# A graph-attention layer with its steps reordered on three engines, its self loop's sum on VectorE and two scalings on ScalarE

## What is computed

```python
x_l = x @ W_l + b_l
x_r = x @ W_r + b_r
e_emb = ea @ W_e                              # edges, and one self loop per node with the mean weight
m = leaky_relu(x_l[src] + x_r[tgt] + e_emb, 0.2)
logits = einsum(m, att)
alpha = softmax(logits) over the edges of a target
out = gelu(segment_sum(alpha * x_l[src]) + bias)
h = out + x
h = (h - mean(h)) * rsqrt(var(h) + 1e-5) * ln_w + ln_b     # the inner norm
x = layernorm(x + h)                                       # its scaling is left to the last layer
```

## Time and profile before

| | |
|---|---|
| median of 3 runs | 3335.7 us (3334.68 to 3337.22) |
| profiled execution: its time | 3335.34 us |
| profiled execution: its span | 3333.5 us |
| TensorE, VectorE, ScalarE, GpSimd busy | 78%, 80%, 60%, 57% of the span |
| mean granted TensorE clock | 0.903 |
| DMA | 611.76 MB, mean 184 GB/s |

### The profile page before, as it was taken

How to read it: one execution, slowest core, us unless ns; L and a number is a source line. 1 busy time by engine, 2 the same in 40 slices (tenths; PEclk the granted TensorE clock), 3 DMA queues, 4 the chain that set the end, 5 groups by cost and what they waited for, 6 DMA issues and landing times. The chain is left out here.

```text
span 3333.5 us, 45939 instructions
## 1 busy us (share of the span) xinstructions
PE 2612.3 (78%) x14227; PEld 1767.1 (53%) x14227; DVE 2674.7 (80%) x3290; ACT 2007.4 (60%) x3334; POOL 1912.3 (57%) x1771
## 2 busy tenths in 40 slices
PE   7899999869999968888886989999999853435510
PEld 3466666646666646656654556666666642224300
DVE  6599999969999969999995467788778765999910
ACT  0177777646556649899895666666766653545500
POOL 4477777433333337777773555555555105777776
PEclk9999999989999989999997999999999955566855
DMA  7467667556666647777774456776776656985211
GB/s 209 111 191 221 221 220 222 190 179 199 201 197 198 198 152 230 229 235 231 230 237 122 121 147 172 191 181 178 193 183 178 161 130 194 280 275 172 84 39 40
DMA packets 495084, 611.76 MB, mean 184 GB/s; under 512 B 66866, under 2 KB 284652, under 8 KB 494717
## 3 DMA queue, kind: packets, MB, share of 16 engines
q1 hardware_dynamic: 433030, 495.63, 49.1%
q0 software_dynamic: 56480, 111.88, 12.7%
q10 hardware_dynamic: 5334, 1.32, 0.2%
HBM read 391.94 MB, written 220.55 MB: 184 GB/s over the span
## 5 line engine op out<-in xcount | busy, mean ns | idle before, releaser
L1294 POOL DMA_INDIRECT g_xd_xs<-table_x,dst_row x196 | 227.8, 1162 | 338.8 <-PE g_psT L1361 245.7
L1801 POOL DMA_INDIRECT f_rows<-table_x,src_row x196 | 229.2, 1169 | 231.9 <-POOLq L1216 172.5
L775 POOL DMA_INDIRECT c_xs<-table_x,src_row x196 | 185.4, 946 | 303.4 <-PE c_psT L916 250.2
L765 POOL DMA_INDIRECT c_xs<-table_h,src_row x196 | 220.5, 1125 | 120.5 <-issue 78.4
L497 POOL DMA_INDIRECT xs<-in_x,src_i x196 | 227.1, 1159 | 86.5 <-issue 55.5
L482 POOL DMA_INDIRECT xd<-in_x,dst_i x196 | 216.6, 1105 | 94.8 <-issue 47.9
L1294 POOL DMA_INDIRECT g_xd_xs<-table_x,src_row x196 | 221.0, 1128 | 59.8 <-issue 59.8
L1808 POOL DMA_INDIRECT out<-f_rows,end_i x196 | 197.4, 1007 | 62.5 <-issue 62.5
L1853 PE MATMUL f_psT<-w_ident,f_rows 128*128 128x128 f32 x196 | 48.7, 395 | 220.3 <-DVE f_rows L1946 220.3
L765 POOL DMA_INDIRECT c_xd<-table_h,dst_row x196 | 185.8, 948 | 59.8 <-issue 59.8
L1366 PEld LDWEIGHTS g_psP<-w_center,g_turns 128*128 128x128 f32 x1568 | 185.5, 192 | 26.6 <-ACT g_turns L1520 13.1
(11 more groups left out here) (333 smaller groups left out, 8643.8 us busy)
## 6 DMA issues: line engine op xcount, KB each, us to landing
g_share<-shares SPq DMA_DIRECT2D x196, 192.0 KB
xn<-in_x SPq DMA_DIRECT2D x49, 512.0 KB
table_x<-xo SPq DMA_DIRECT2D x49, 512.0 KB
table_x1b<-xb SPq DMA_DIRECT2D x49, 512.0 KB, 4.9
c_xn<-table_x SPq DMA_DIRECT2D x49, 512.0 KB
table_h<-c_xo SPq DMA_DIRECT2D x49, 512.0 KB
c_xn<-table_h SPq DMA_DIRECT2D x49, 512.0 KB
c_x1r<-table_x1b SPq DMA_DIRECT2D x49, 512.0 KB
```

Source lines behind the costliest of these rows:

```text
L765: pool.indirect_dma_start(out=quarters(rows[:, s, :])[j], out_offset=None, in_=table, in_offset=edge_index(columns, now.n, j)).then_inc(la ...
L775: pool.indirect_dma_start(out=quarters(xs[:, s, :])[j], out_offset=None, in_=table, in_offset=edge_index(h.src_row, now.n, j)).then_inc(sr ...
L1294: pool.indirect_dma_start(out=quarters(xd_xs[:, s, k, :])[j], out_offset=None, in_=table, in_offset=edge_index(columns, now.n, j)).then_in ...
L1801: pool.indirect_dma_start(out=quarters(rows[:, n, :])[j], out_offset=None, in_=table, in_offset=edge_index(h.src_row, n, j)).then_inc(src_ ...
```

## The change

- The matmul with w_lr and its semaphore `zs_ready` are gone. VectorE makes low = x w_r (psZ, bank 0) + b_self + values of the destination, which already hold x w_l + b_l; so b_self is now made with b_r alone. zsl is then max(0.2 low, low), read from SBUF. ScalarE's pass for `low` is gone.
- n1 of the two node blocks is made by ScalarE in eight passes of 128 columns (`scale_block`), n1 of the edge block stays on VectorE. n1_ready is split into n1n_ready and n1e_ready.
- The order on TensorE, ScalarE and VectorE is another. TensorE starts a step with the node transposes; logits come after both centrings; the next edges' transposes before the second edge centring. ScalarE scales between the Gelus and nodeT, makes the squares before affe, and loads the table of Ln and Exp after affe. On VectorE pre1 comes before the scan, pre2 of the nodes before the sums, and the softmax's parts are spread.
- The logits wait for `args_ready` and `shares_ready`, where they waited for `m_cols` and `d_cols`.
- A number `behind` appears, with value 0, so `d` = `c` and `lead` = `lag`.

```diff
-                                                in1=h.blr[:, :], op0=ALU.mult, op1=ALU.add))
+                                                in1=h.col("b_r"), op0=ALU.mult, op1=ALU.add))
...
-        lag, ring, runs = 11, 12, 7
+        lag, ring, runs, behind = 11, 12, 7, 0
+        lead = lag - behind
...
 TensorE
+                if is_tile(d):
+                    pe.wait_ge(node_landed[d % 4], 16 * (d // 4 + 1))
+                    pe.wait_ge(e_kept, min(c + 1, STEPS))
+                    wait(pe, affn_ready, min(g2, STEPS))
+                    for k in range(2):
+                        ins = turned_rows(psT[:, k, :], xn[:, d % 4, k, :])
+                    ins.then_inc(n_turned, 1)
                 if now:
...
-                if last:
-                    pe.wait_ge(zl_ready, c)
...
-                if now:
-                    pe.wait_ge(node_landed[c % 4], 16 * (c // 4 + 1))
-                    for k in range(2):
-                        ins = turned_rows(psT[:, k, :], xn[:, c % 4, k, :])
-                    ins.then_inc(n_turned, 1)
                 if is_tile(g1):
...
+                if last:
+                    pe.wait_ge(zl_ready, c)
+                    pe.wait_ge(zsl_ready, c)
+                    wait(pe, a_kept, c - 1)
+                    done = (c - 1 - runs - 1) // runs + 1
+                    wait(pe, args_ready, done)
+                    done = (c - 1 - runs - 2) // runs + 1
+                    wait(pe, shares_ready, done)
...
                 if is_tile(g2):
-                    pe.wait_ge(n_kept, min(c + 1, STEPS))
+                    pe.wait_ge(n1n_ready, g2 + 1)
+                    wait(pe, n_kept, min(d + 1, STEPS))
...
-                    nc.tensor.matmul(psZ[:, 1, :], h.w_lr[:, :], edgeT[:, c % 2, 0, :],
-                                     start=True, stop=True).then_inc(zs_ready, 1)
...
+                if is_tile(c + 1):
+                    wait(pe, n_kept, min(d + 1, STEPS))
+                    wait(pe, affn_ready, min(g2 + 1, STEPS))
+                    turn_edges(c + 1)
                 if is_tile(e2):
                     pe.wait_ge(affe_ready, e2 + 1)
                     centred(psU[:, 0, :], affT[:, 2, :]).then_inc(fe_ready, 1)
-                if is_tile(c + 1):
-                    pe.wait_ge(n_kept, c + 1)
-                    wait(pe, affn_ready, g2 + 1)
-                    turn_edges(c + 1)
...
 ScalarE
+            def scale_block(k):
+                for j in range(4):
+                    ins = nc.scalar.activation(quarters(n1[:, k, :])[j], quarters(pre1[:, k, :])[j], ACT.Copy,
+                                               scale=rstd1[:, 4 * k + j:4 * k + j + 1])
+                return ins
...
+                if is_tile(g2):
+                    act.wait_ge(rstd1_ready, g2 + 1)
+                    wait(act, n1n_turned, g2)
+                    scale_block(0)
+                    act.wait_ge(rstd1_ready, g2 + 1)
+                    wait(act, n1n_turned, g2)
+                    scale_block(1).then_inc(n1n_ready, 1)
...
-                if is_group(g1):
-                    nc.scalar.preload_act_table_set(LN_EXP)
...
                 if is_group(g1):
...
+                    nc.scalar.activation(sq1[:, a:b, :], pre1[:, a:b, :], ACT.Square).then_inc(sq1_ready, 1)
                 if is_tile(e2):
...
                 if is_group(g1):
...
-                if now:
-                    act.wait_ge(zs_ready, c + 1)
-                    wait(act, zsl_ready, c)
-                    nc.scalar.activation(low[:, :], psZ[:, 1, :], ACT.Identity, bias=h.x2b_self[:, :],
-                                         scale=0.2).then_inc(low_ready, 1)
...
+                    nc.scalar.preload_act_table_set(LN_EXP)
...
 VectorE
-                if is_group(g2):
-                    a, b = blocks_of(g2)
-                    dve.wait_ge(rstd1_ready, g2 + 1)
-                    wait(dve, n1n_turned, min(g2, STEPS))
-                    wait(dve, n1e_turned, e2)
-                    scaled(n1[:, a:b, :], pre1[:, a:b, :], rstd1[:, 4 * a:4 * b], b - a, n1_ready)
...
+                if is_tile(e2):
+                    dve.wait_ge(rstd1_ready, g2 + 1)
+                    wait(dve, n1e_turned, e2)
+                    scaled(n1[:, 2:3, :], pre1[:, 2:3, :], rstd1[:, 8:12], 1, n1e_ready)
...
+                if now:
+                    dve.wait_ge(z_ready, c + 1)
+                    dve.wait_ge(v_kept, c + 1)
+                    wait(dve, zsl_ready, c)
+                    nc.vector.scalar_tensor_tensor(out=low[:, :], in0=psZ[:, 0, :], scalar=h.b_self[:, :],
+                                                   in1=values[:, c % ring, 1, :], op0=ALU.add,
+                                                   op1=ALU.add).then_inc(low_ready, 1)
...
-                    nc.vector.scalar_tensor_tensor(out=zsl[:, :], in0=psZ[:, 1, :], scalar=h.b_self[:, :],
-                                                   in1=low[:, :], op0=ALU.add, op1=ALU.max).then_inc(zsl_ready, 1)
+                    nc.vector.scalar_tensor_tensor(out=zsl[:, :], in0=low[:, :], scalar=0.2, in1=low[:, :],
+                                                   op0=ALU.mult, op1=ALU.max).then_inc(zsl_ready, 1)
```

More of the change, by code:

```diff
@@ L1274, in blocks_of, with run_at @@
         def blocks_of(g):
-            return 0 if is_tile(g) else 2, 3 if is_tile(g - lag) else 2
+            return 0 if is_tile(g) else 2, 3 if is_tile(g - lead) else 2
         def is_group(g):
-            return 0 <= g < STEPS + lag
-        def run_at(c, behind):
-            s, k = divmod(c - behind, runs)
+            return 0 <= g < STEPS + lead
+        def run_at(c, later):
+            s, k = divmod(c - later, runs)
             return s if k == 0 and 0 <= s < runs else None
@@ L1318, in _ @@
                     load_weights(c + 1)
-                    load_nodes(c + 1)
+                if is_tile(c + 1 - behind) and c + 1 > behind:
+                    load_nodes(c + 1 - behind)
                 e = c + 1 - lag
@@ L1491, in _ @@
                 now, last = is_tile(c), is_tile(c - 1)
-                g1, g2, e1, e2 = c - 1, c - 2, c - 1 - lag, c - 2 - lag
+                d, e1, e2 = c - behind, c - 1 - lag, c - 2 - lag
+                g1, g2 = d - 1, d - 2
+                s1, (a, b) = run_at(c, runs + 1), blocks_of(g1)
                 if is_tile(g1):
@@ L1501, in _ @@
                     nc.scalar.activation(ge[:, :], agg[:, e1 % 2, :], ACT.Gelu, bias=h.col("g_bias")).then_inc(ge_ready, 1)
[L1502 to L1505 removed]
+                if is_tile(g2):
[5 more added lines that the diff above has]
+                    scale_block(1).then_inc(n1n_ready, 1)
+                if is_tile(d):
+                    act.wait_ge(n_turned, d + 1)
+                    wait(act, y_ready, d - 1)
+                    nc.scalar.activation(nodeT[:, d % 2, :, :], psT[:, :, :], ACT.Copy).then_inc(n_kept, 1)
                 if now:
@@ L1680, in _ @@
                     nc.vector.tensor_tensor(v, v, share[:, e0 % 2, 1:3, :], ALU.mult).then_inc(weighed, 1)
+                if is_tile(e2):
+                    dve.wait_ge(rstd1_ready, g2 + 1)
+                    wait(dve, n1e_turned, e2)
+                    scaled(n1[:, 2:3, :], pre1[:, 2:3, :], rstd1[:, 8:12], 1, n1e_ready)
+                if s2 is not None:
+                    running_sum(s2)
+                if is_tile(e0):
+                    v = values[:, e0 % ring, :, :]
                     dve.wait_ge(weighed, e0 + 1)
                     nc.vector.tensor_tensor(v[:, 0, :], v[:, 0, :], v[:, 1, :], ALU.add).then_inc(summed, 1)
+                if is_tile(g1):
+                    wait(dve, n1n_ready, g1)
+                    wait(dve, sq1_ready, g1)
+                    dve.wait_ge(en_ready, g1 + 1)
+                    dve.wait_ge(node_landed[g1 % 4], 16 * (g1 // 4 + 1))
+                    nc.vector.tensor_tensor(pre1[:, 0:2, :], psP[:, :, :], xn[:, g1 % 4, :, :],
+                                            ALU.add).then_inc(pre1n_ready, 1)
+                if is_tile(e1):
+                    wait(dve, n1e_ready, e1)
+                    wait(dve, sq1_ready, g1)
+                    dve.wait_ge(ee_ready, e1 + 1)
+                    dve.wait_ge(x2e_landed[e1 % 4], 16 * (e1 // 4 + 1))
+                    nc.vector.tensor_tensor(pre1[:, 2, :], psU[:, 0, :], x2e[:, e1 % 4, :],
+                                            ALU.add).then_inc(pre1e_ready, 1)
+                if is_tile(e0):
+                    v = values[:, e0 % ring, :, :]
                     dve.wait_ge(summed, e0 + 1)
@@ L1713, in _ @@
                                                    op1=ALU.add).then_inc(zw_ready, 1)
-                if is_group(g1):
-                    a, b = blocks_of(g1)
-                    dve.wait_ge(sq1_ready, g1 + 1)
-                    wait(dve, lnv1_ready, g1)
-                    sums(var1[:, 4 * a:4 * b], sq1[:, a:b, :], var1_ready)
-                s = run_at(c, runs + 1)
-                if s is not None:
```

(17 more changed lines are left out.)

137 lines of the change are left out of this document (52 added, 85 removed).

## The result

| | before | changed |
|---|---|---|
| median of 4 runs, us | 3336.11 (3334.68 to 3337.22) | 3238.03 (3237.07 to 3240.71) |
| ratio | | 0.9708 [0.9691, 0.9724] |
| span of the profiled execution, us | 3333.5 | 3236.0 |
| mean granted clock | 0.903 | 0.905 |

A forecast was written before the change was run, and what follows sets the result against it. The prediction held that the order of work, not any engine's load, set the 16.84 us step. Savings of 75.0 (full steps), 20.4 (steps 2 to 11) and 3 (tail), together 98.4 us, gave 3237 us, range 3222 to 3272.

The forecast's parts named there:

- The ring of the kernel before: Old full step: order, not load, sets 16.84 us, a chain over TensorE (6.72), ScalarE (7.09) and VectorE (3.03).
- Full steps: Steps 12 to 48: 15.25 us each for 16.84; with softmax pairs, 75.0 us saved of 647.55.
- the two rooms called tight: New full step: zl ready 0.1 us before the value products need it, Gelu done at 17.7 for the centring at 17.9.
- TensorE's floor: TensorE's work in a new full step without waits: 15.95 less 0.86, so 15.09 us.
- The w_lr product goes: 0.86 us: TensorE, self loop: removing this product lowers the work of a full step by 0.86 us, to 15.09.
- ScalarE's scalings: Eight node scalings added on ScalarE, 2.5 us a step; its work becomes 14.0 us, below the floor, so hidden.
- The rival of ScalarE as the ring: Scalings without overlap and late affn: full steps about 15.6 us, early ones 14.2, kernel 3256 us; chance 0.16.
- Table loads: ScalarE: the logarithm's load, 1.28 us, moves behind affe; nothing added, no extra load for the squares.
- Steps 2 to 11: Ten early steps of nodes and logits: 13.6 us each, 137.65 for 158.02 us with one softmax pair, 20.4 saved.
- The ring is node centring ..., pre2n, sums, Ln, ...: Steps 2 to 11: chain on through Gelu, scalings, nodeT, values, alike and affn, 13.5 us, above TensorE's floor of 12.82.
- Softmax steps: Each run's two longer steps: extra work falls from 4.79 to 1.65 us a pair, bounds 1.2 and 4.8.
- it stood behind it: Twelve edge-only tail steps: pre1e no longer waits behind the scan, 0.26 us a step, 3 us in all.

The follow-up runs named there:

- order_only_2: Changed kernel with w_lr product, ScalarE's low and VectorE's node scaling back, leaving the new order alone: 3263.68 us, ratio 0.9788.
- zsl_early: Changed kernel with zsl moved ahead of pre2n on VectorE: 3243.56 us, ratio 0.9725.
- gelu_first: Changed kernel with node scaling on VectorE, zsl before pre2n except in the maximum's step, Ln and Exp behind the next step's Gelus: 3234.03 us, ratio 0.9700.
- scale_back_2: Changed kernel with only the node scaling moved back to VectorE: 3240.06 us, ratio 0.9715; as scale_back on the chip with slow transfers 3464.6 us, 0.9791.
- half_y: Changed kernel without the second of the two node products with w_l, from the third tile on: 3237.12 us, ratio 0.9706.
- self_only_2: Kernel before with only the self loop changed (no w_lr product, low on VectorE): 3374.3 us, ratio 1.0118.

## Why the prediction was right, and where it was not

**The ring of the kernel before: right in the main, wrong in its last stretch.** The step was set by the order, not by a load. order_only_2 shows it: the same work in another order takes 15.80 us a step for 16.84. But I closed the ring through the last products. It closed through zl: the last products take 1.79 us behind a wait (in the early step below, to 1903.15), in the earlier trace rows it is 1.86 to the value products, and the 0.07 us are their wait for zl. The sum of 16.84 could not show it, since it runs from a row to the same row a step later.

**Full steps: right, 15.21 for 15.25 us**, and the two rooms called tight closed: zl for the value products, Gelu for the centring. zsl_early cuts the ring through zl and meets the one through the Gelu at the same 15.21; that the one through zl would hold it alone is what its rows add up to, and was not run. Without both the step is 14.96 (gelu_first). So TensorE's floor, put at 15.09, was about 0.3 too high: the last products and the value products take 1.72 us each start to start where nothing is waited for, and I had taken 1.86 and 1.87 for them from the earlier trace rows.

**The step "The w_lr product goes: 0.86 us": right as a lowering of the floor, incomplete as a price.** With low on VectorE it costs 39 us in the old order, a third of it in plain full steps and part of the rest at the lower clock; in the new order it gives 24. The order alone gives 72 us, so the parts do not add up, and the self loop's change does not pay without the order. My working priced low at 0.74 us inside VectorE's load and asked only in the new order what stands behind it.

**ScalarE's scalings: hidden, as said.** 2.43 us on ScalarE leave the steps as they are with 1.21 us on VectorE. They brought a wait that my list had not: VectorE's pre1 waits for them, 1.81 us in the step shown. The changed kernel's waits, 2000 to 2560 us (total, times, longest):

```profile
DVE g_pre L1698 <- ACT g_n L1490: 45.5, 31, 1.9
...
PEld g_psP L1368 <- ACT g_turns L1504: 23.6, 36, 3.4
```

The first costs nothing, since scale_back_2 has it not and the same steps. The second, 0.66 us on average, is the Gelu at the tight room; it is a wait of the weight load, which otherwise runs ahead, and in plain steps the products behind it start at most 0.1 us late. The rival of ScalarE as the ring fell: affn waits for the transposes, not for ScalarE. The rule of the Trainium skill beside that rival (ScalarE: Activation LUTs, Rules for kernel authors) is borne out in the price, 2.43 us for 1.21, and decides nothing here, since neither place lies on the ring that closes a plain step.

**Table loads: right.** No third load comes with the squares, and what follows a load starts 1.29 us after its start (2439.34 - 2438.05). The drain of about 1.38 us that the Trainium skill gives (same page, What ACT_TABLE_LOAD costs) is in no row of after either.

**Steps 2 to 11: 14.02 for 13.6 us, 3 of the 20.4 us not had.** The step that failed is "The ring is node centring ..., pre2n, sums, Ln, ...": I followed pre2n only to the sums, not to the last products. A plain early step of the changed kernel, TensorE:

```profile
1897.83 2.05 PE L1368 MATMUL g_psP<-w_center,g_turns 128*128 128x128 f32 x16 [0.43 <-ACT g_turns L1533]
...
1901.36 1.96 PE L1475 MATMUL g_psP<-g_nodeT,w_w_l 128*128 128x512 f32 x4 [0.61 <-DVE g_pre L1742]
```

and VectorE:

```profile
1899.99 1.23 DVE L1742 TENSOR_TENSOR g_pre<-g_psP,g_xn 128x1024 f32<-128x1024 f32 x1 [1.15 <-PE g_psP L1368]
```

In a full step the edge centring (0.89 us) stands between the next edges' transposes and the last products and covers the 1.23 us of pre2n. Here it is absent, TensorE waits 0.61 us, and the ring is TensorE's own from the last products to the inner transposes, affn, node centring, pre2n: 14.02 us. half_y cuts the last products and gets 13.77.

**Softmax steps: 1.87 for 1.65 us a pair**, within the bounds. **Tail: 0.1 us for 3.** The failed step is "it stood behind it" of pre1e and the scan, priced at 0.26 us a step. A step of the tail took 9.30 us for 9.34. TensorE there, answering to the earlier trace rows:

```profile
2624.45 2.08 PE L1368 MATMUL g_psU<-w_center,g_turns 128*128 128x128 f32 x8 [2.15 <-ACT g_turns L1509]
```

and VectorE:

```profile
2626.73 0.69 DVE L1705 TENSOR_TENSOR g_pre<-g_psU,g_x2e 128x512 f32<-128x512 f32 x1 [1.30 <-PE g_psU L1368]
```

With the scan out of its way pre1e still starts 0.20 us after the centring's end at 2626.53. Of the 0.26 us that I read as a queue behind the scan 0.20 were the hand-over from TensorE to VectorE, and 0.06 could be had.

**Not priced: the layer's start (3.9 us) and the last layer (1.0 us).** 3.1 of the 3.9 us are there by the first node Gelu, at 1823.3 us for 1826.4. The layer before ends at the same time in both (1793.83 and 1793.81 us). From its end to the first node Gelu it is 32.6 us in the kernel before, 31.1 in self_only_2, 30.3 in order_only_2 and 29.5 in the changed kernel: the self loop's change has 1.5 us of the 3.1 alone, the order 2.3. The 1.0 us of the last layer stays unexplained.

## What to carry to other kernels

Follow each late operand to every engine that reads it, and ask for each kind of step, full, early and tail, what covers the wait: one missing instruction of 0.9 us uncovered a wait of 0.6. A removed operation pays by what it frees on the ring that closes the step; put where it has no room, its replacement can cost more than the whole saving (39 us here), so try parts in both orders. Look at the row right behind a product, too: one that starts 0.10 us after another engine's result is waiting for it, even if no idle time is shown. When a step is near its floor, two or three rings close at once, and shortening one of them shows nothing until the others are cut too.

## What was not expected of the hardware

- The same kernel took 3336.1 us beside the changed one, 3335.1 and 3335.6 us on two chips used later and 3545.7 us on another, at a lower mean granted clock (scale_back 0.887 for 0.903) and with a store that took over 30 us to free its buffer. Which of the two comes first is not shown. A gain on compute is not the same gain there: 0.9791 for 0.9715 with the same kernel.
- An edit that takes a product from TensorE and lengthens its waits can cost clock: in self_only_2 the last products ran at a granted clock of 0.50 behind a wait of 3.43 us, and took 3.75 us for 1.96.
- From the modelled end of TensorE's centring to VectorE's read of its result it is 0.10 us in a full step (2434.46 to 2434.56) and 0.20 in the tail (2626.53 to 2626.73), where nothing else is in the way. The 0.26 us of the earlier trace rows were no sign of a long queue.
- The last products (x4) take 1.72 us start to start in a row without waits (2430.37 to 2432.09 in gelu_first), 1.79 where they begin behind a wait (1901.36 to 1903.15 in the changed kernel), and 1.86 in the earlier trace rows, where the row behind them also waits for zl. A step's work summed from rows with waits is too long by some 2% (15.09 for 14.8 us).
